# A two-layer attention kernel on one core: late units pass two key blocks to the sums of the weights directly, and five edits of the order

## The reference, cut to what matters

```python
# layer 0, for each of 4 sequences; ctx is the context, 16 heads of 32 channels
Q, K, V = q @ Wq.T + bq, ctx @ Wk.T + bk, ctx @ Wv.T + bv
att = softmax(Q K^T / sqrt(32)) ; out = (att V) @ Wo.T + bo
x = layernorm(out + q) * gamma0 + beta0
# layer 1
Q_phi, K_phi = elu(x), elu(ctx)
KV = K_phi^T @ ctx                      # 512 x 512
Z = 1 / (Q_phi . K_phi.sum(tokens) + 1e-6)
out = layernorm(x + (Q_phi @ KV) * Z) * gamma1 + beta1
```

## Time and profile before

| | us |
|---|---|
| median of three runs | 1574.0 |
| the profiled execution | 1583.65 |
| its span, first to last instruction | 1581.9 |
| TensorE matmul busy | 1477.9 (93%) |
| VectorE busy | 1317.8 (83%) |
| GpSimd busy | 1269.1 (80%) |
| ScalarE busy | 932.3 (59%) |

### The profile page before, as it was taken

The page is one execution under the profiler, slowest core; times in us unless marked ns, Lnnn a source line. Parts: engine busy times, 40 slices in busy tenths (PEclk is TensorE's granted clock), DMA queues, the critical chain, the costliest instruction groups (busy, mean ns, idle before and its releaser), DMA issues.

```text
span 1581.9 us, 29154 instructions
## 1 busy us (share of the span) xinstructions
PE 1477.9 (93%) x9976; PEld 1015.8 (64%) x9976; DVE 1317.8 (83%) x2448; ACT 932.3 (59%) x1892; POOL 1269.1 (80%) x1069
## 2 busy tenths in 40 slices
PE   8998999999999999999999999999999898998986
PEld 5775776667757667566666767667665555555654
DVE  5768878887788898788999889987978889998874
ACT  3445555665666656556665656655756555665563
POOL 0457777777799988877988989987969899899863
PEclk9999999999999999899999999999999999999998
DMA  7646645246344515333552532445241221301000
GB/s 255 198 132 187 227 154 165 87 122 202 98 125 131 147 47 174 97 124 90 188 145 86 167 90 94 136 143 150 90 124 50 72 62 45 103 27 37 26 16 34
DMA packets 136754, 183.70 MB, mean 116 GB/s; under 512 B 19104, under 2 KB 69408, under 8 KB 136608
## 3 DMA queue, kind: packets, MB, share of 16 engines
q1 hardware_dynamic: 134352, 179.22, 37.4%
q10 hardware_dynamic: 2256, 2.63, 0.5%
HBM read 125.18 MB, written 56.62 MB: 115 GB/s over the span
## 4 chain that ended last, share of the span: by engine, by line
PE 53%; DVE 14%; POOL 13%; issue 10%; DMA 5%; ACT 3%; SPq 1%; POOLq 0%; DVEq 0%; ACTq 0%
PE acc L732 9%; PE score L697 9%; PE scoreT L711 9%; PE misc L790 7%; POOL pair_sum L1327 7%; DVE maxes L1071 5%; PE misc L786 4%; PE misc L827 4%; DVE pair_sum L1111 4%; PE misc L802 4%; PE misc L819 3%; DMA stage<-ctxT_in 1%; POOL pair_sum L1336 1%; PE acc L748 1%; ACT p_ring L894 1%
## 5 line engine op out<-in xcount | busy, mean ns | idle before, releaser
L894 ACT ACTIVATE p_ring<-scoreT 128x512 f32<-128x512 f32 x1024 | 595.8, 593 | 465.6 <-PE scoreT L711 459.5
L1071 DVE TENSOR_REDUCE maxes<-score 128x1 f32<-128x512 f32 x1024 | 672.2, 676 | 123.2 <-PE score L697 120.3
L1327 POOL TENSOR_TENSOR pair_sum<-p_ring 128x512 f32<-128x512 f32 x504 | 664.8, 1327 | 129.6 <-ACT p_ring L894 76.3
L697 PE MATMUL score<-k_stack,q_stack 96*128 96x512 f32 x1024 | 535.1, 523 | 36.4 <-DVE maxes L1071 34.2
L711 PEld LDWEIGHTS scoreT<-q_stack,k_stack 104*128 104x128 f32 x2048 | 388.0, 194 | 177.4 <-ACT p_ring L894 89.8
L711 PE MATMUL scoreT<-q_stack,k_stack 104*128 104x256 f32 x2048 | 430.9, 292 | 29.5 <-ACT p_ring L894 24.2
L697 PEld LDWEIGHTS score<-k_stack,q_stack 96*128 96x128 f32 x1024 | 196.0, 191 | 194.1 <-issue 88.7
L732 PE MATMUL acc<-p_ring,v_sb 128*32 128x256 f32 x4096 | 260.3, 397 | 0.0
L1111 DVE TENSOR_TENSOR pair_sum<-pair_sum 128x512 f32<-128x512 f32 x189 | 234.2, 1239 | 24.9 <-POOL pair_sum L1327 24.7
L1336 POOL TENSOR_TENSOR pair_sum<-pair_sum 128x512 f32<-128x512 f32 x189 | 254.7, 1347 | 0.0
L732 PEld LDWEIGHTS acc<-p_ring,v_sb 128*32 128x32 f32 x4096 | 123.6, 113 | 90.6 <-issue 11.3
(11 more groups left out here) (129 smaller groups left out, 1485.1 us busy)
## 6 DMA issues: line engine op xcount, KB each, us to landing
q_stack<-q_dram SPq DMA_DIRECT2D x189, 128.0 KB, 2.6
k_stack<-k_dram SPq DMA_DIRECT2D x93, 256.0 KB, 5.7
w_parts<-w_dram SPq DMA_DIRECT2D x45, 512.0 KB, 5.6
k_dram<-kept_parts SPq DMA_DIRECT2D x28, 512.0 KB, 3.1
q_dram<-kept_parts SPq DMA_DIRECT2D x27, 512.0 KB, 3.1
ctx_nat<-ctx_in SPq DMA_DIRECT2D x32, 256.0 KB, 3.7
v_sb<-v_dram SPq DMA_DIRECT2D x15, 512.0 KB, 4.3
tiles<-x_in SPq DMA_DIRECT2D x27, 256.0 KB, 3.5
```

What stands on the lines that cost most here:

```text
L697: pe.matmul(score[k % 3][:], q_stack[0:SPLIT, unit % NQ, j, t * P:(t + 1) * P], k_stack[0:SPLIT, group_of[unit] % 2 * QUAD + j, h * HALF:( ...
L894: act.activation(p_ring[:, n % NP, h * HALF:(h + 1) * HALF], scoreT[k % 2][:], ACT.Exp, scale=SCALE).then_inc(A["exped"], 1)
L1071: dve.reduce_max(maxes[:, unit % 2, t, j, h:h + 1], score[k % 3][:], AX.X).then_inc(V["maxed"], 1)
L1327: pool.tensor_tensor(pair_sum[:, place_of_pair(pair), cols], p_ring[:, (n - 1) % NP, cols], p_ring[:, n % NP, cols], ALU.add).then_inc(L[" ...
```

## The change

1. Units 46 to 62 (`SHORT` = 46) sum three pairs instead of four; their last two key blocks go into the divisor by direct matmuls in the second visit, as all blocks of unit 63 do. In these units the high half of pair 2 is added by GpSimd (`add_last`) and not by VectorE.
2. `keep_low` is a tick later, and `put_kept` with it, except for the first two projections.
3. From tick 272 on a staged piece is given five ticks to land instead of three before it is split.
4. In sequences 2 and 3 both halves of the queries are projected first. Projections from there on may start every 10 ticks (before 9.5), with a deadline 36 ticks later (before 56).
5. outT has 21 places instead of 19; `unused` goes.
6. The dot is booked two ticks after the transposition T or later and writes over the features; A waits for it in the plan, the features of the next tile don't.

```diff
-    NQ, NP, NO, NX = 3, 7, 19, 3
+    NQ, NP, NO, NX = 3, 7, 21, 3
+    SHORT = 3 * UB - 2
+    def pairs_of(unit):
+        return SLOTS if unit < SHORT else SLOTS - 1 if unit < SUMMED else 0
...
-        projections += [*(("Q", g, cp) for cp in range(2 if b == 1 else 1) for g in groups), *(("V", b, kb) for kb in blocks),
+        projections += [*(("Q", g, cp) for cp in range(2) for g in groups), *(("V", b, kb) for kb in blocks),
                         *(("K", g, 0) for g in groups), *(("K", g, 1) for g in groups),
-                        *(("V", b, kb + KT // 2) for kb in blocks), *(("Q", g, 1) for g in groups if b > 1)]
+                        *(("V", b, kb + KT // 2) for kb in blocks)]
...
-                return FIRST if n < 3 * UB // 2 else 280 + 19 * (n - 3 * UB // 2) // 2
+                return FIRST if n < 3 * UB // 2 else 280 + 10 * (n - 3 * UB // 2)
-                return earliest(kind, i) + 56 if earliest(kind, i) > FIRST else FIRST
+                return earliest(kind, i) + 36 if earliest(kind, i) > FIRST else FIRST
...
-            return use, k + 3
+            return use, k + (3 if k < UT * UB + UT else 5)
...
-            phi_of[i] = book("phi", "DVE", max(grow_of[i], end_of.get(("T", i - 1), FIRST), dot_of.get(i - 1, FIRST)) + 1, 10, i)
-            dot_of[i] = book("dot", "DVE", phi_of[i] + 1, 13, i)
+            phi_of[i] = book("phi", "DVE", max(grow_of[i], end_of.get(("T", i - 1), FIRST)) + 1, 10, i)
+                dot_of[i] = book("dot", "DVE", end + 2, 13, i)      # behind T
...
-                    put = send("put_kept", end + 1, turn_of_kept[what], 2, False)
+                    put = send("put_kept", end + 2, turn_of_kept[what], 2, False)
...
-                if unit >= SUMMED:
+                if unit >= SHORT:
                     for s in range(VISIT):
                         n = VISIT * v + s
+                        if n % KT < 2 * pairs_of(unit):
+                            continue
                         for j in range(QUAD):
                             mm = pe.matmul(acc[j * DK:(j + 1) * DK, CH:2 * CH], ones[:, 0:DK],
                                            p_ring[:, n % NP, j * CH:(j + 1) * CH], start=False,
...
+                if unit >= SHORT:
+                    pe.wait_ge(L["run_last"], unit + 1 - SHORT)
...
-                    if n - NP < KT * SUMMED:
-                        act.wait_ge(L["paired"], 2 * ((n - NP) // 2 + 1))
+                    last, kt = divmod(n - NP, KT)
+                    if kt // 2 < pairs_of(last):
+                        act.wait_ge(L["paired"], 2 * (pairs_until(last) + kt // 2 + 1))
...
+            def add_last(unit):
+
+                whole, part = (pair_sum[:, place_of_pair(unit, p), HALF:2 * HALF] for p in (0, 2))
+                pool.wait_ge(L["paired"], 2 * pairs_until(unit + 1))
+                pool.wait_ge(V["run_high"], highs_until(unit + 1))
+                pool.tensor_tensor(whole, whole, part, ALU.add).then_inc(L["run_last"], 1)
```

94 lines of the change are left out of this document (54 added, 40 removed).

## The result

The changed kernel is slower. Its median is 1592.15 us against 1574.58 us of the kernel before, timed beside it; the ratio is 1.0098, with a 95% interval of 1.007 to 1.0127. The forecast was 1550, faster, and its range ended at 1577. The profiled execution of the changed kernel took 1593.24 us (span 1591.6), 1 us above its median; that of the kernel before lay 9 us above its own.

The account below looks back on a forecast made before the run. TensorE was taken to bound the kernel until 1200 us, then the divisor's additions on busy GpSimd and VectorE; terms -17.4 + 1 - 6 - 2 + 2 - 1 - 1 = -24.4 us from 1574.0 gave 1550, range 1533 to 1577.

Parts of the forecast that it names:

- the price of part 4: Queries together: shorter put waits and fewer weight reloads, the moved data still in time; -1 us (-4 to +5).
- The last sentence of the prediction: The prediction fails if the late stretch hangs on the tiles' step order, not the divisor's additions; no size given.
- part 3 -6 forecast: Staged context pieces: two more ticks cover ScalarE's longest wait for them; -6 us (0 to -8).
- Part 1: Late units: fewer additions on GpSimd and VectorE, more TensorE matmuls; together -17.4 us, with +1 for units 46 to 48.
- rival (a): VectorE's hold-ups beside GpSimd go as well, "issue" gives 12 to 20 us more: 1534; chance 0.13.
- The terms of the divisor's additions: Late stretch of the chain: GpSimd's additions (L1327) give -13.2 us, VectorE's high additions (L1111) -16.4 us.
- Part 2: Low parts a tick later: VectorE's filled waits give -2 us (0 to -10), later puts cost +2 (0 to +10).
- Parts 5 and 6: 21 outT places bring 0; the dot behind T frees the next tile's features earlier; -1 us (-3 to +2).
- (b): Projections: the single place of the parts becomes the wait, 14 late puts, +10 instead of +2: 1560; chance 0.17.
- (c): Late units: TensorE becomes the bound, its 14.8 us paid in full and the relief returns nothing: 1583; chance 0.12.
- (d): Planner fills the freed GpSimd ticks, relief equals the 0.87 us, stage and puts cancel: 1571 to 1577; chance 0.05.
- The marks that the prediction set: Signs of being right: late TensorE idle under 7%, stage waits near 2 us, L1152 under 20 us.

Follow-up runs that it names:

- e2: The kernel before with part 4 alone (query halves first, new times and deadlines): 1592.01 us, ratio 1.0084.
- g3: The changed kernel with the six transfers that stack the keys of group 12 issued 12 ticks later: 1583.6 us.
- g2: The changed kernel without part 3, so three ticks for a staged piece again: 1581.12 us.
- i4: The kernel before with parts 1 and 4 only: 1583.93 us, ratio 1.0052.
- m1: i4 with the tiles of sequence 2 started 14 ticks later: 1566.7 us.
- e3: The kernel before with part 3 alone, five ticks for a staged piece: 1571.12 us, ratio 0.9962.
- i1: The kernel before with parts 1, 2 and 3: 1545.17 us, ratio 0.9797.
- e6: e1 with the high half of pair 2 left on VectorE instead of GpSimd: 1566.79 us.
- e4: The kernel before with part 2 alone, low parts and their puts a tick later: 1567.29 us, ratio 0.993.
- f1: The changed kernel without part 4: 1552.6 us, ratio 0.9842.
- e1: The kernel before with part 1 alone: 1551.46 us, ratio 0.9831.
- k1: The changed kernel with the stacking of the keys of groups 9 and 12 issued 12 ticks later: 1559.27 us.
- f2: The changed kernel without part 1: 1590.91 us, ratio 1.0075 to the kernel before.
- h2: e1 with all high halves of units 46 to 62 added by GpSimd, none by VectorE: 1561.27 us.

## Why the prediction was wrong

**What failed is the price of part 4**: "-1 (-4 to +5)". It costs 13 us alone and 39.5 us inside the change. The step looked at transfers only. Three things in it failed.

- It had no term for TensorE. The order moves pieces into ticks in which TensorE has no room, though the earlier trace rows had it idle for no more than 4.1% before 1200 us: 8.6 us more in ticks 464 to 512 and 3.5 more in 736 to 752, and nothing won where they are missing (e2). This is most of what part 4 costs alone, and its first half is there in every trace: ticks 448 to 544 take 138.0 to 139.6 us in the eight kernels with part 4's order, and 129.7 to 133.6 in the twelve without it.
- "put, fetched and landed in some 41 ticks (59 us), which is enough" asked only whether the moved data come in time. They do. What else moves with the order was not asked: the puts of the last keys, from ticks 697 to 714 to 720 to 737, past tick 731, at which six fetches are put into the same queue. The step named SyncE's queue for part 2 ("stacking transfers there ahead of it"), and didn't look at it for part 4. Price by g3: some 8 us, and only in the whole change: with part 4 alone (e2), or without part 3 (g2), the put and the next high part fall so that at most 2.8 us are waited.
- "go ahead of O, T and A, whose order isn't pressed there" took the tiles for filler whose place costs nothing. Their place decides what stands beside the scores of the late units: i4 against m1, 17 us. The last sentence of the prediction ("if the late stretch hangs on the order of the tiles' steps and not on the divisor's additions") had it as a way to fail; it hangs on both, and it was given no price.

What the step said of the put waits came true: those for queries fell from 6.1 to 2.3 us (e2). It was worth nothing.

**The sum was made of parts that don't add.** Each was priced against the trace of before, and the runs confirm most of them in that form: part 3 -6 forecast, -6 measured (e3). But 1 + 4 is 20 us worse than their sum (i4), 1 + 2 + 3 is 11 us short of it (i1), and part 3 turns to +11 inside the change (g2). The parts change the places of the same chains. A range from the bounds of the parts alone (1533 to 1577) was too narrow for that.

**Part 1** was right in its mechanism and undersized: -24 instead of -16.4. The excess fits rival (a): VectorE's held-up time went from 78 to 39 us. Of the extra 12 to 20 us that (a) gave, some 8 came. That the high addition on VectorE is the dear one is shown by e6. The terms of the divisor's additions were right in direction: L1111 is at 1.266 us in the changed kernel (forecast: below 1.3).

**Part 2** was sized wrong, -11 against 0 (-2 and +2). "VectorE isn't the bound before 1200 us" is wrong for the first 160 ticks, where some 8 us of it fell (e4). The row was there: the longest of the waits, 7.9 us, was read and said to lie at the start, and the mean over 1160 us decided instead.

**Parts 5 and 6** were put at -1; f1 against i1 suggests +7. This stays open.

**The rivals.** (b) named the right resource, the one place of the parts, and gave +10 for fourteen puts late by 0.7 us. It came as one wait of 9.5 us, and for another reason: fetches ahead of it in the queue, not a late low part. (c), the case on the slower side, is refuted by e1: part 1 alone gains 24 us where (c) had it cost 14.8. The kernel became slower for a reason that no rival held. (d) is refuted by e1 too. That the changed kernel ended up on the slower side, for which 0.12 was given, is no success of (c).

**The marks that the prediction set.** TensorE's idle share in the late stretch "under 7%" is 7.5% in the changed kernel and 5.3% in e1. ScalarE's waits for pieces "near 2 us" are 6.8 us. The waits of L1152 "under 20 us" are 22.6 us, and 17.7 in e4. Puts in ScalarE's waits are 16.6 us together (10.7 and 5.9) and passed the 8 us that were given for (b).

**Left open.** The staged piece and the held-up features around 790 to 840 us went away together with a shift of most later chains (k1), so 24 us of that run aren't shared out. Which step of the early tiles costs in the late units is not known. Of the 37.6 us in ticks 448 to 768, 10.9 weren't followed up. The changed kernel without part 2, and the new order with the old deadlines, have no run.

## What to carry to other kernels

Where a planner books everything, an edit of the order is priced by what comes to lie under it: list every transfer whose tick moves, and look up what else is put into the same queue at its new place; whether data come in time for their user is only half of the question. Gains that were read one by one from the trace of before don't add when each of them shifts the same filler work; measure the parts alone and the whole without each, as e1, f1 and f2 do here, before the sum is believed. And where VectorE is held up beside a busy GpSimd, moving one addition over to GpSimd can pay (e6, 15 us) and moving the next can cost (h2, 10 us). An engine's busy share says whether work can be moved to a stretch: where TensorE is at 99%, what is moved there is paid in full (e2).

## What the runs showed of the hardware

- VectorE's instruction with two inputs can be held up far beyond the GpSimd instruction at hand: 0.68 us became 8.43, beside six of them without a gap, and it ended 0.55 us after the last. The Trainium skill ("SBUF — State Buffer", section "Summary: rules for kernel authors") says that where VectorE has two inputs in SBUF and GpSimd reads it, "the second one to issue **fully blocks** until the first finishes". By that the hold-up should end with one instruction of 1.26 us. In the kernel before, 117 of VectorE's instructions of this kind (128x512, both inputs in SBUF) take 1.2 us or more. 74 of them, all under 1.9 us, end while GpSimd's next one is under way, and that one then takes 1.53 to 1.75 us instead of 1.28, as if it were blocked in its turn: these agree with the rule. None of the nine over 2.5 us does so; they end in a gap of GpSimd's or beside its instruction on one column. There the measurement decides. What makes a hold-up of the one kind or the other isn't known.
- By the rule's direction the addition moved to GpSimd (part 1) should have harmed VectorE. It gained 15 us (e1 against e6), since it also takes away an instruction that was itself held up to 1.59 us on average.
- A put of the parts, which has a median of some 3.2 us to its landing and took at most 7.8 in the kernel before, took 9.18 us behind nine fetches that were issued in the 4.4 us before it, 8.7 behind the same nine in g2, and 5.3 with only the three of the queries ahead (g3). A staged piece took 12.38 us behind six and a few more. The Trainium skill ("DMA: Bandwidth & Descriptors", section "Queues, rings and completion order") says that each DMA engine takes the descriptors of one issuer's queue in the order of its ring; these times agree with it.
- A TensorE left without work costs more than the wait's length. It stood still for 8.08 us up to 1095.14; from 1092.1 to 1098.8 the granted clock was 0.50 (1.2 of 2.4 GHz), and the visit of 32 matmuls that starts in it took 3.31 us instead of 1.86.
